# Down products in three one-pass terms, upper halves by a rounding write, and loads in another order, in a decoder layer with a mixture of experts on one core

## The reference, cut to what matters

```python
x = x + _L0_attn_ref(_layernorm(x), ...)
x = x + _L0_xattn_ref(_layernorm(x), ctx_1024, ctx_1024, ...)
x = x + _L0_ffn_ref(_layernorm(x), ...)
...
scores = sigmoid(xf @ gate_w.T)
_, sel = top_k(scores + expert_bias, 2)
top_scores = take_along_axis(scores, sel, axis=-1)
def body(acc, ew):
    e, wu, wd = ew
    w_t = sum(where(sel == e, top_scores, 0.0), axis=-1)
    h = square(relu((xf * w_t[:, None]) @ wu.T))      # wu: 256 x 128
    return acc + h @ wd.T                             # wd: 128 x 256
```

## Time and profile before

| what | value |
|---|---|
| median of 3 runs | 135.36 us (135.22 to 135.91) |
| profiled execution, device time | 135.17 us |
| profiled execution, span from first to last instruction | 133.4 us |
| granted TensorE clock | 1.00 throughout |
| PE busy | 120.1 us, 90% of the span, 1668 instructions |
| PEld busy | 103.1 us, 77% |
| DVE busy | 98.5 us, 74%, 328 instructions |
| ACT busy | 59.5 us, 45% |
| POOL busy | 37.6 us, 28% |

### The profile page before, as it was taken

The page is one execution under the profiler, slowest core; times in us unless marked ns, Lnnn a source line. Parts: engine busy times, 40 slices in busy tenths (PEclk is TensorE's granted clock), DMA queues, the critical chain, the costliest instruction groups (busy, mean ns, idle before and its releaser), DMA issues.

```text
span 133.4 us, 4223 instructions
## 1 busy us (share of the span) xinstructions
PE 120.1 (90%) x1668; PEld 103.1 (77%) x1668; DVE 98.5 (74%) x328; ACT 59.5 (45%) x132; POOL 37.6 (28%) x71
## 2 busy tenths in 40 slices
PE   6989869989998995687799999999999999999991
...
GB/s 95 254 252 269 410 69 0 7 5 0 5 5 2 5 5 0 0 2 5 0 7 0 0 5 2 160 157 135 226 0 0 5 59 297 0 44 0 0 2 39
DMA packets 4867, 8.44 MB, mean 63 GB/s; under 512 B 344, under 2 KB 3824, under 8 KB 4208
## 3 DMA queue, kind: packets, MB, share of 16 engines
...
...
## 4 chain that ended last, share of the span: by engine, by line
PE 48%; DVE 31%; DMA 10%; issue 6%; SPq 2%; ACT 1%; DVEq 0%
PE ps L901 22%; PE ps L890 17%; DMA c_sb<-ctxt 5%; DVE low L528 5%; DVE feat L517 4%; DMA wup_sb<-w_up 4%; DVE negm L522 4%; DVE onat L536 2%; DVE topi L580 2%; PE ps L867 2%; DVE wtop L627 1%; DVE topv L573 1%; DVE vals L545 1%; PE ps L859 1%; DVE nat L506 1%
## 5 line engine op out<-in xcount | busy, mean ns | idle before, releaser
L669 DVE SCALAR_TENSOR_TENSOR rel<-ps,wb_sb 128x512 f32<-128x512 f32 x32 | 21.7, 686 | 13.0 <-PE ps L890 8.6
L901 PE MATMUL ps<-wdn_sb,hid 128*128 128x128 f32 x256 | 30.3, 275 | 0.0
L901 PEld LDWEIGHTS ps<-wdn_sb,hid 128*128 128x128 f32 x256 | 29.4, 192 | 0.0
L452 ACT ACTIVATE hid<-rel 128x512 f32<-128x512 f32 x32 | 20.0, 635 | 16.3 <-DVE rel L669 13.5
L890 PE MATMUL ps<-xhi,whi 128*128 128x256 f32 x64 | 19.2, 301 | 0.1
L890 PE MATMUL ps<-xhi,wlo 128*128 128x256 f32 x64 | 17.8, 278 | 0.0
L890 PE MATMUL ps<-xlo,whi 128*128 128x256 f32 x64 | 17.8, 278 | 0.0
L890 PEld LDWEIGHTS ps<-xhi,whi 128*128 128x128 f32 x64 | 12.1, 188 | 1.1 <-issue 1.0
L315 POOL TENSOR_SCALAR rstd<-mv 128x2 f32<-128x2 f32 x12 | 2.6, 219 | 34.2 <-DVE mv L478 34.0
L890 PEld LDWEIGHTS ps<-xlo,whi 128*128 128x128 f32 x64 | 12.1, 189 | 0.0
L890 PEld LDWEIGHTS ps<-xhi,wlo 128*128 128x128 f32 x64 | 12.0, 188 | 0.0
(11 more groups left out here) (115 smaller groups left out, 210.3 us busy)
## 6 DMA issues: line engine op xcount, KB each, us to landing
...
```

The source lines that it names most:

```text
L452: nc.scalar.activation(hid[:, a % 3, :], rel[:, a % 2, :], ACT.Square).then_inc(done["sq"], 1)
L669: nc.vector.scalar_tensor_tensor(rel[:, a % 2, :].rearrange("p (c t) -> p c t", c=2), psum("up", a).rearrange("p (c t) -> p c t", c=2), 0. ...
L901: last = mm(acc_ps[:, D * t:D * (t + 1)], hid[:, a % 3, 2 * P * half + P * t:2 * P * half + P * (t + 1)], wdn_sb[:, e, half, :], start=(e ...
```

## The change

1. **Down products.** `down.a` no longer multiplies in plain fp32. `wdn_sb` is split like `w_up`: `wdh` on ACT writes `wdhi` (F32R), `wdl` on POOL writes `wdlo`, four pieces each. The squared activations are split too: `hhi.a` on DVE copies `hid` to F32R, and `hlo.a` subtracts, on POOL, except for every fourth expert (`a % 4 == 3`), where DVE does it (`hlod.a`). Six matmuls of 256 columns replace the four of 128. The weights are now the stationary operand, so `acc` holds features on partitions and tokens in columns.
2. **Turned back by chunk.** After a chunk's eighth down, `acct` on ACT copies `acc` to `yT`, and `turn` on PE transposes it (two transposes); `fin` reads that.
3. **Upper halves by a rounding write.** `wtop` and `xtop` are gone. ACT writes `whi` and `xhi` straight from source, rounding on the write to F32R; POOL subtracts. `xhi` is a second ACT copy from PSUM ahead of `xn3T`.
4. **Buffers.** `rel` gets three buffers, `hid` six (in the memory of `nat`), `hhi` and `hlo` three each. `wb_sb` is gone: the routing weights lie in `wup_sb` and `wdn_sb`, once those are split.
5. **Loads.** SP: x 0-1, the identity, x 2-3, x 4-7, context 0-3, context 4-7. ACT: `wqkv` first, then as before.
6. **Order and banks.** All tables are new.

The diff, cut to its core:

```diff
-HIGH = 0xFFFFF000
+HS, LS = 3, 4
...
-        rel = sb("rel", [P, 2, 4 * P])
-        hid = sb("hid", [P, 3, 4 * P])
+        rel = sb("rel", [P, 3, 4 * P])
+        hid = nat[:].rearrange("p t c j d -> p (t c j d)").rearrange("p (k n) -> p k n", n=4 * P)
+        hhi = sb("hhi", [P, HS, 4 * P], F32R)
+        hlo = sb("hlo", [P, HS, 4 * P], F32R)
...
+        def lower_done(engine, a):
+            if a % LS == LS - 1:
+                engine.wait_ge(hlo_dve, a // LS + 1)
+            else:
+                engine.wait_ge(hlo_pool, a - a // LS + 1)
...
@@ sync
             sp.dma_start(x_sb[:, 0:2, :], xv[:, 0:2, :]).then_inc(ld_x0, 16)
-            sp.dma_start(wqkv_sb[:], w_qkv).then_inc(ld_wqkv, 16)
+            sp.dma_start(con[:, 0:C_FWD], consts[:, 0:C_FWD]).then_inc(ld_id, 16)
             sp.dma_start(x_sb[:, 2:4, :], xv[:, 2:4, :]).then_inc(ld_x1, 16)
+            sp.dma_start(x_sb[:, 4:TILES, :], xv[:, 4:TILES, :]).then_inc(ld_x, 16)
             sp.dma_start(c_sb[:, 0:4, :], cv[:, 0:4, :]).then_inc(ld_c0, 16)
-            sp.dma_start(x_sb[:, 4:TILES, :], xv[:, 4:TILES, :]).then_inc(ld_x, 16)
...
@@ gpsimd
+                if name == "hlo" and a % LS != LS - 1:
+                    upper_done(pool, a)
+                    pool.wait_ge(done["sq"], a + 1)
+                    if a >= HS:
+                        pool.wait_ge(full["down"], a - HS + 1)
+                    nc.gpsimd.tensor_tensor(hlo[:, a % HS], hid[:, a % 6], hhi[:, a % HS].bitcast(F32), ALU.subtract)
...
@@ scalar
-            act.dma_start(con[:, 0:C_FWD], consts[:, 0:C_FWD]).then_inc(ld_id, 16)
+            act.dma_start(wqkv_sb[:], w_qkv).then_inc(ld_wqkv, 16)
...
+                    nc.scalar.copy(xhi[:, a % 2, :], psum(name, a)[:, 0:2 * P]).then_inc(xhi_ready, 1)
...
+                if name == "acct":
+                    act.wait_ge(full["down"], EXPERTS * (a + 1))
+                    nc.scalar.copy(yT[:], psum("acc", a)[:, 0:2 * P]).then_inc(done[name], 1)
...
@@ vector
+                if name == "hhi":
+                    dve.wait_ge(done["sq"], a + 1)
+                    if a >= HS:
+                        dve.wait_ge(full["down"], a - HS + 1)
+                    nc.vector.tensor_copy(hhi[:, a % HS], hid[:, a % 6]).then_inc(hhi_ready, 1)
+                if name == "hlod" and a % LS == LS - 1:
+                    upper_done(dve, a)
+                    nc.vector.tensor_tensor(hlo[:, a % HS], hid[:, a % 6], hhi[:, a % HS].bitcast(F32), ALU.subtract)
...
@@ tensor
-                            last = mm(acc_ps[:, D * t:D * (t + 1)], hid[:, a % 3, 2 * P * half + P * t:2 * P * half + P * (t + 1)],
-                                      wdn_sb[:, e, half, :], start=(e == 0 and t == 0 and half == 0),
+                    for i, (w, r) in enumerate(((wdhi, hhi), (wdlo, hhi), (wdhi, hlo))):
+                        for half in range(2):
+                            last = mm(acc_ps[:, 0:2 * P], w[:, e, half, :], r[:, a % HS, 2 * P * half:2 * P * (half + 1)],
```

More of the change, by code:

```diff
@@ L45 @@
 C_LEN = C_IOTA + 8
-MATMULS = ("cent", "spread", "xt", "cdft", "cproj", "qkv", "score", "pt", "vtr", "pv", "vt2", "wo", "dft", "qp", "corr", "g", "ov", "y2",
+MATMULS = ("cent", "spread", "turn", "xt", "cdft", "cproj", "qkv", "score", "pt", "vtr", "pv", "vt2", "wo", "dft", "qp", "corr", "g", "ov", "y2",
            "xt3", "gate", "wt", "up", "down")
-EVACS = ("cent", "spread", "xt", "cdft", "cproj", "qkv", "pt", "vtr", "pv", "vt2", "wo", "dft", "qp", "corr", "g", "ov", "y2", "xt3", "gate",
+EVACS = ("cent", "spread", "acct", "xt", "cdft", "cproj", "qkv", "pt", "vtr", "pv", "vt2", "wo", "dft", "qp", "corr", "g", "ov", "y2", "xt3", "gate",
          "wt", "up", "sq", "fin", "rs1", "rs2", "rs3", "nm3")
@@ L54 @@
     "PE": """
[L55 to L62, removed]
@@ L91 @@
[L91 to L94 removed]
+        warm.12.0 xt.0.0 cent.0.0 xt.1.0 qkv.0.0 qkv.0.1 qkv.1.0 cdft.0.0 qkv.1.1 cdft.1.0 cproj.0.0 vtr.0.0 xt.2.0 xt.3.0
+        cent.0.1 vtr.0.1 score.0.0 score.0.1 qkv.2.0 vtr.1.0 qkv.2.1 vtr.1.1 qkv.3.0 score.1.0 score.1.1 pt.0.0 pt.0.1 pt.0.2
@@ new lines @@
+        xt3.0.0 gate.0.0 g.2.0 up.0.0 ov.2.0 up.1.0 xt3.1.0 y2.2.0 wt.0.0 up.2.0 gate.1.0 g.3.0 spread.0.0 ov.3.0 up.3.0 xt3.2.0
+        y2.3.0 up.4.0 wt.1.0 up.5.0 up.6.0 up.7.0 up.8.0 down.0.0 up.9.0 up.10.0 gate.2.0 down.1.0 down.2.0 down.3.0 up.11.0
+        up.12.0 down.4.0 xt3.3.0 down.5.0 wt.2.0 up.13.0 down.6.0 down.7.0 up.14.0 up.15.0 down.8.0 up.16.0 down.9.0 gate.3.0
+        down.10.0 up.17.0 down.11.0 up.18.0 down.12.0 down.13.0 wt.3.0 turn.0.0 up.19.0 down.14.0 up.20.0 up.21.0 down.15.0
@@ new lines @@
+    "POOL": """
+        rs1.0.0 rs1.1.0 rs1.2.0 vpar.0.0 vpar.0.1 rs1.3.0 x12.0.0 x12.1.0 vpar.1.0 vpar.1.1 x12.2.0 x12.3.0 wlo.0.0 vpar.2.0
+        vpar.2.1 wlo.0.1 wlo.0.2 wlo.0.3 wdl.0.0 wdl.0.1 wdl.0.2 wdl.0.3 vpar.3.0 vpar.3.1 rs2.0.0 rs2.1.0 rs2.2.0 mix.0.0
+        mix.1.0 rs2.3.0 rs3.0.0 mix.2.0 xsp.0.0 rs3.1.0 mix.3.0 xsp.1.0 rs3.2.0 hlo.0.0 hlo.1.0 hlo.2.0 xsp.2.0 rs3.3.0 hlo.4.0
+        hlo.5.0 hlo.6.0 hlo.8.0 hlo.9.0 hlo.10.0 xsp.3.0 hlo.12.0 hlo.13.0 hlo.14.0 hlo.16.0 hlo.17.0 hlo.18.0 hlo.20.0 hlo.21.0
+        hlo.22.0 hlo.24.0 hlo.25.0 hlo.26.0 hlo.28.0 hlo.29.0 hlo.30.0""",
@@ L695, in released @@
                 elif name == "acc":
+                    pe.wait_ge(done["acct"], a + 1)
+                elif name == "turn":
                     pe.wait_ge(done["fin"], a + 1)
```

198 lines of the change are left out of this document (115 added, 83 removed).

## The result

| | before | after |
|---|---|---|
| median of the runs taken together | 135.62 us (135.22 to 135.91, 4 runs) | 144.3 us (143.68 to 146.39, 4 runs) |
| profiled execution, and its span | 135.17 us, 133.4 | 144.04 us, 142.2 |
| first rel of DVE | 73.14 | 81.39 |
| busy share PE / DVE / POOL | 90% / 74% / 28% | 84% / 88% / 52% |

The ratio is 1.0614, with a 95% interval of 1.0562 to 1.0665. Every median here is over all executions; the ratios leave out those more than 1.5% above the fastest of their kernel, whose granted clock was mostly lower (here the one of 146.39). The forecast was 139.0 with a range up to 143.5: the direction is right, the time lies outside.

What follows compares the result with a forecast made beforehand. The prediction took DVE to bound attention and PE the experts. First rel 76.4, DVE's own work 42.6 and holds of 9.4 and 3.8 gave 132.2; the tail made span 137.1, plus 1.8 outside: 139.0 us, range 128.5 to 143.5.

Steps and rivals of the forecast that it cites:

- part 1: Everything ahead of DVE's first rel: it would move from 73.14 to 76.4 us.
- The moved steps, +6.4: Ahead of the first rel: DVE steps of later chunks, such as qp.3 and top.3, move there and add 6.4 us.
- Loads, -1.2: At the start: the new load order brings DVE's first qkv step, at 10.41, forward by 1.2 us (0 to 2).
- The gate, +1.5: Ahead of the first rel: pick.1 waits for gate.1, now behind wt.0's four ACT copies, adding 1.5 us.
- Gaps I cannot place, +0.6: Ahead of the first rel: an allowance of 0.6 us for gaps without a known place.
- wtop and xtop, -2.3: Ahead of the first rel: wtop with its wait and the first xtop leave DVE, saving 2.3 us.
- Parts 2 and 3: Expert stage: DVE's own work of 42.6 us, then holds by POOL of 9.4 and 3.8; last hlod at 132.2.
- Part 4, the tail: After the last hlod: half an hlo, last down, acct, turn, fin and 2.3 us to the end; span 137.1.
- PE stays the bound: Expert stage: hhi does not wait for POOL and PE remains the limit; 128.5 us (127 to 130), chance 0.20.
- Held, but packed tightly: Expert stage: DVE fills every hold with rels, so exclusion costs only its sum; 132.5 us (131 to 136), chance 0.10.
- The doubt about the order: Attention stage: it could pack worse, the first rel coming after three chunks' work; up to 3 us in each case.
- the signs: From 77 us: DVE 80% busy or more, hhi maximum above 1.2; PE's share some 80%. First rel after 79 means wrong.

Runs made afterwards that it cites:

- Experiment 4: The changed kernel with the eight copies whi and wdh moved behind vtr.1.1 in ACT's list: 142.66 us, ratio 1.0454.
- experiment 8: The changed kernel with the six loads back in the order of the kernel before: 144.36 us, ratio 1.0628.
- experiments 5 and 11: The kernel before with the new order of the loads alone, run on two occasions: 138.8 us (ratio 1.0181), then 137.7 us (ratio 1.0122).
- experiment 6: The kernel before with the rounding write alone (wtop and xtop gone, xhi and xlo with four buffers): 133.95 us, ratio 0.9882.
- experiment 1: The changed kernel with POOL's subtraction hlo replaced by two short pow operations of 128x2: 137.66 us, ratio 1.0017.
- experiment 3: The changed kernel with all 32 subtractions hlo on DVE behind their hhi, none on POOL: 147.93 us, ratio 1.0873.
- experiments 2: The changed kernel with all 32 copies hhi moved from DVE to ACT: 139.24 us, ratio 1.0213.
- experiment 7: The changed kernel with whi and wdh later on ACT, and hhi on ACT for three experts of four: 137.2 us, ratio 1.0111.

## Why the prediction was wrong, and where it was right

**The step that failed is part 1, the first rel: 76.4 predicted, 81.39 measured, 5.0 us late.** The direction and the mechanism in the expert stage were right; the time ahead of it was mis-summed. Its sum implied 67.7 us of DVE work and 8.7 of standing (63.15 + 6.4 - 1.85 of wtop and xtop; the rest). The profile has 69.10 and 12.29. Experiment 4, without the stall at w_up, lets the miss be taken apart, with 68.75 and 10.86 up to 79.61. Each figure is from one profiled execution:

- *The moved steps, +6.4*: DVE worked 1.05 us more than that in experiment 4. The largest piece that can be named is vals, a two-source step whose longest takes 727 ns instead of 282. Where the rest lies is not shown: the moved steps were priced from a few rows each.
- *Loads, -1.2*: less than half of it came. The first qkv step stood at 10.38 in experiment 4 and 10.26 in the changed kernel, 10.41 before, and DVE stood only 0.5 us less up to that point (6.7 against 7.2). The loads themselves were worth what was forecast: with the loads of before the same list reaches that step at 11.39 (experiment 8), 1.1 later. But the new list puts both pairs of statistics ahead of the step, and in the new order of the loads the first x tiles land some 0.5 us later (DVE begins with them between 3.8 and 4.1 instead of 3.3 to 3.4); neither stood in the sum. On the kernel before this edit cost 1.2 to 1.8% (experiments 5 and 11).
- *The gate, +1.5*: measured 1.08 (the row at 79.39). *Gaps I cannot place, +0.6*: five gaps behind PE of 0.28, 0.42, 0.24, 0.39 and 0.67 in experiment 4, 2.0 together, and some 0.4 more than before of pieces too small for a row. The two terms together came out 1.4 us short.
- *Not in the sum at all*: ACT's wait for w_up with four whi and a vkey behind it, and the lower clock that followed, together 1.8 us (81.39 against 79.61). The prediction moved work onto ACT, called ACT's room sufficient, and never asked what the work at the head of ACT's list would wait for, although the row was there: wtop waited 0.45 us for that load, and whi takes its place.
- *wtop and xtop, -2.3*: alone they gave 1.67 (experiment 6): DVE worked 2.06 us less, and lost part of it again in front of the first rel (1.07 us for `wb_sb`, 0.50 before). The forecast also took those 0.50 off.

The pieces of 1.05, 0.7, 1.4 and 1.8 add up to the 5.0.

**Parts 2 and 3, own work and holds: right.** From the first rel to the end of the last hlod there were to be 55.8 us; there are 56.2 (81.39 to 137.57). DVE's own work was to be 42.6; without the holds it is 42.4 (experiment 1). The holds were to take 13.2; DVE is busy for 55.2 us in the changed kernel, 12.8 more than in experiment 1. Some 10 of them are on hhi, and experiment 3 gives 10.8 by another way. Their spread came out otherwise than forecast: only two of the eight hlod were held (1.18 and 1.65 us), and one xn (1.44 for two). The price of hhi, 0.33 from start to start and a median near 0.41, was right too (420 ns).

**Part 4, the tail**: 4.9 predicted, 4.6 measured (137.57 to 142.2), right. So 5.0 of the 5.1 us by which the span is longer than forecast (142.2 against 137.1) are part 1's.

**The rivals.** "PE stays the bound" is out: its condition was an hhi that POOL does not hold, and hhi goes to 1503 ns. "Held, but packed tightly" is out: POOL stood 20.9 us for hhi. The doubt about the order, "up to 3 us", pointed at the right place with too small a size. Of the signs, the 98% of DVE from 81.4 us on, the hhi and the first rel after 79 came as described. PE stood less in front of the downs than the 0.2 to 0.4 us per expert: 3.9 us for all 32, 2.9 of them for hlo, and its share from 90 to 110 was 86%, not 80.

The Trainium skill, page "SBUF — State Buffer", section "SBUF: two separate sides", states an exclusive lock, held for a whole instruction, between GpSimd and a VectorE operation in a 2-port mode or with two SBUF inputs. The runs agree for POOL's subtraction: a held copy ends 0.29 us after it. They do not agree for every POOL instruction: beside 48 instructions on two columns of 0.75 to 0.81 us each, with SBUF sources, no hhi took more than 560 ns (experiment 1).

**What the change is worth by parts.** The rounding write is a gain (0.988). The new downs save PE time, and with the copy off DVE the expert stage, from the first rel to the end of the last hlod, takes 50.7 and 50.6 us instead of 56.2 (experiments 2 and 7). But the order that feeds them starts the experts 8 us later, 6.8 in experiment 7. From the first rel to the end of the span that kernel needs 55.3 us and the one before 60.3: 5.0 won, 6.8 lost. The downs were not tried on the order of before; whether they gain there is open. Of the kernels run, the one before with the rounding write is the best, at 133.95 us without the new loads and 134.26 or 134.62 with them, which these runs can't tell apart.
